# Tap positions and bias as two further products of the offset convolution, and four sampled tiles in flight

## The chip, the cores and the metric

The kernel runs on one core of a Trainium2 chip. The core has five engines that run their own instruction streams: TensorE (PE, matrix products, writing to the eight PSUM banks), VectorE (DVE), ScalarE (ACT), GpSimd (POOL) and SyncE (SP, which here only issues DMAs). They meet through semaphores. The metric is the device time of one execution in microseconds, as the median of several runs; less is better. A profile is taken in a separate execution.

## The reference, cut to what matters

Four layers run one after the other on an image batch `x` of shape (16, 32, 32, 32), each with a group norm before it and added to `x`: a mixture of experts on 2x2 patches, a deformable 3x3 convolution, a state-space layer, a depthwise 7x7 convolution with an MLP. The change lies in the second:

```python
om = _conv3x3(x, w_om, b_om)                # 27 channels: 9 dy, 9 dx, 9 masks
o1, o2, m = jnp.split(om, 3, axis=1)
offset = jnp.concatenate([o1, o2], axis=1)
mask = jax.nn.sigmoid(m)
dy = offset[:, 0::2]
dx = offset[:, 1::2]
base_y = (jnp.arange(H)[None, :, None] - 1 + ky.reshape(K2, 1, 1)).astype(jnp.float32)
base_x = (jnp.arange(W_)[None, None, :] - 1 + kx.reshape(K2, 1, 1)).astype(jnp.float32)
py = base_y[None] + dy
px = base_x[None] + dx
y0 = jnp.floor(py)
x0 = jnp.floor(px)
...                                         # four corners gathered, weighted, summed, times the mask
out = jnp.einsum('bckhw,ock->bohw', sampled, w.reshape(CO, C, K2))
```

So a sampling position is: a convolution with `w_om`, plus a bias `b_om` per channel, plus the place of the tap, which is the pixel's row (or column) plus the tap's own offset.

## The kernel before

The 16 images are worked in four **steps** of four images (NS = 4), and the partitions hold 4 images x 32 channels. Layers are staggered: while step s is in the deformable convolution, the experts of step s+1 and the state-space and depthwise layers of step s-1 run beside it. `order(step)` is a hand-made schedule: it gives every piece of work a place between 0 and 32, the numbers of the step's 32 gather tiles ("slots"), and each engine runs its own pieces in that one order. A piece late on one engine so holds back everything behind it on that engine.

**The deformable layer.** `head_a(a)` prepares the images of a pass a (passes 0, 1 and 2 are image 0, image 1, and images 2 and 3 of the first step; passes 3, 4 and 5 are whole steps). Its parts in order:

- `l1_norm`: DVE writes the normed image, with a border, to `xpad`.
- `l1_conv`: PE, nine products (one for each tap of the 3x3 window) with `w_om`, 108 output rows, of 512 columns for half an image's pixels (two pieces of 256 and one of 512 in pass 0); ACT copies the bank to `omt` (L1141).
- `l1_table`: PE transposes `xpad`, ACT copies, SP stores the table of corners to memory, from where POOL gathers.
- `l1_om`: PE transposes `omt` (L1764) so that pixels lie on the partitions; DVE adds the table `bb` of places and bias (L1451) and clips the positions to 0..33 (L1456) in `cw`.
- `l1_index` and `l1_share`: DVE floors the positions, makes the row numbers `idx` for the gather, and the corner weights `cw` from the fractions and the mask, whose tanh ACT makes (L1163).

`l1_conv` is written in pieces (`pieces(a)`): three in pass 0, two in each other pass, 13 in all. Passes 1 and 2 lie in the first step, at slots 3.2 to 5.5 and 11.9 to 15; passes 3 to 5 at slots 23.9 to 29 of the steps 0 to 2, for the next step. `load_conv` on DVE adds the bias to `bb` once (L1325).

**The tiles.** For each tile of 128 pixels of one image POOL issues nine indirect DMAs into `gt` (L1055), a ring of GRING = 4 places: the gathers of tile t wait until DVE has written `sm` of tile t-4. DVE's `sample` multiplies with the corner weights (L1508), adds twice (L1510), and writes the sampled tile to `sm` (L1516). `sm` is a ring of two places: this last instruction waits until PE has transposed the tile t-2 (`B1.filled(dve, "sampled", s, t - 2)`). PE's `turn` (L1772, at slot t+1) transposes `sm` into PSUM bank 3, ACT copies it to `st` (L1173), and `dcn` (L1783) multiplies with the weights after each group of tiles.

1152 gathers are issued in all (128 tiles of nine), from 78.2 us of the profiled execution to 1983.5 us.

## Time and profile before

| | |
|---|---|
| runs without a profile, us | 1748.33, 1746.49, 1748.08 |
| median, us | 1748.08 |
| span of the profiled execution, first to last instruction, us | 2176.8 |
| mean granted TensorE clock in it | 0.801 |
| PE / weight loads / DVE / ACT / POOL busy, us | 1392.0 / 595.6 / 953.2 / 526.5 / 1190.0 |
| DMA traffic | 123.70 MB, mean 57 GB/s |

The profiled execution is 428.7 us longer than the median. No record of what lies around its span stands in the profile, so the span is taken as its own time. Times of single instructions come from it; the sum of waits in it is not that of a run without a profile. In the granted clock 1.0 is 2.4 GHz and 0.5 is 1.2 GHz. A row of a timeline gives start, duration, engine, source line, operation, output<-input, the count, and in brackets how long the engine had been idle and what ended that ("issue": nothing that the profile shows; "remote": something it can't name).

### The profile page before, as it was taken

The numbers are of one execution on the slowest core, as the hardware profiler recorded it, in microseconds if no ns is written. First come the engines' busy times: TensorE is split into PE (matmuls) and PEld (weight loads), VectorE is DVE, ScalarE is ACT, GpSimd is POOL, SyncE is SP. The second block draws the span as 40 slices with busy tenths as digits, with TensorE's granted clock in tenths as the row PEclk, the third lists the DMA queues.
The fourth block names the chain that finished last, engine by engine and source line by source line (L and its number), as shares of the span: only waits on it lengthen the run. The fifth ranks groups of instructions, "written<-read, shape, count | busy, mean of one in ns | idle before, by whom it ended". The sixth has DMA issues, their size and how long they took to land.

```text
span 2176.8 us, 13143 instructions
## 1 busy us (share of the span) xinstructions
PE 1392.0 (64%) x3780; PEld 595.6 (27%) x3780; DVE 953.2 (44%) x1562; ACT 526.5 (24%) x860; POOL 1190.0 (55%) x1393
## 2 busy tenths in 40 slices
PE   4647554496246877863366878855368874386976
PEld 3433212242112333322122333322123321132322
DVE  2424233354341333884532323875323328532564
ACT  1111111121112233211222333211213322132544
POOL 8655446357665555676565454676645566673000
PEclk9868766698567998986577889977678987687987
DMA  5212212132241111222141111222221112110100
GB/s 192 60 48 68 52 40 62 49 90 59 74 101 41 43 44 43 71 66 58 53 113 46 31 40 39 74 65 58 57 76 35 41 44 57 41 58 26 32 5 18
DMA packets 111591, 123.70 MB, mean 57 GB/s; under 512 B 50720, under 2 KB 88224, under 8 KB 111136
## 3 DMA queue, kind: packets, MB, share of 16 engines
q0 software_dynamic: 36864, 75.57, 12.5%
q1 hardware_dynamic: 73600, 43.82, 8.1%
q10 hardware_dynamic: 1056, 3.47, 0.4%
q8 instruction: 31, 0.51, 0.1%
q14 instruction: 40, 0.33, 0.0%
HBM read 99.79 MB, written 9.01 MB: 50 GB/s over the span
## 4 chain that ended last, share of the span: by engine, by line
PE 36%; another core or an unknown queue 27%; DVE 16%; issue 12%; ACT 7%; DMA 1%; SPq 1%; ACTq 0%; DVEq 0%
PE bank L1795 7%; PE bank L1808 7%; PE bank L1721 4%; DVE rb L1599 3%; PE bank L1717 3%; PE bank L1731 3%; DVE gt L1508 3%; PE bank L1752 2%; PE bank L1831 2%; PE bank L1783 2%; PE bank L1817 1%; DVE he L1406 1%; PE bank L1847 1%; PE bank L1772 1%
## 5 line engine op out<-in xcount | busy, mean ns | idle before, releaser
L1055 POOL DMA_INDIRECT gt<-corner_table,idx x1152 | 1135.1, 985 | 783.8 <-DVE sm L1516 392.4
L1795 PE MATMUL bank<-u,wk 128*128 128x512 f32 x512 | 256.7, 648 | 25.6 <-issue 9.6
L1808 PE MATMUL bank<-yg,wts 128*128 128x512 f32 x512 | 241.6, 615 | 46.9 <-ACT yg L1189 30.2
L1406 DVE SCALAR_TENSOR_TENSOR he<-he,bank 128x512 f32<-128x512 f32 (+1 forms) x144 | 90.2, 627 | 275.4 <-remote 88.9
L1721 PE MATMUL bank<-xg,w_sb 128*128 128x512 f32 (+1 forms) x288 | 149.3, 602 | 85.0 <-DVE xg L1397 61.9
L1772 PE MATMUL bank<-cst,sm 128*128 128x128 f32 x384 | 80.0, 322 | 187.0 <-ACT st L1173 79.7
L1540 DVE SCALAR_TENSOR_TENSOR tg<-tg,ae 128x512 f32<-128x512 f32 x64 | 44.5, 696 | 344.3 <-ACT ae L1201 270.9
L1731 PE MATMUL bank<-he,w_sb 128*128 128x512 f32 (+1 forms) x288 | 143.0, 580 | 54.6 <-DVE he L1406 30.9
L1508 DVE TENSOR_TENSOR gt<-gt,bank 128x1152 f32<-128x1152 f32 x128 | 172.5, 1347 | 0.9
L1599 DVE SCALAR_TENSOR_TENSOR rb<-xp,par,rb 128x1024 f32<-128x1024 f32 x124 | 155.1, 1291 | 0.0
L1125 ACT ACTIVATE he<-bank 128x512 f32<-128x512 f32 (+1 forms) x144 | 78.8, 549 | 294.3 <-PE bank L1717 166.7
L1795 PEld LDWEIGHTS bank<-u,wk 128*128 128x128 f32 x512 | 102.5, 208 | 164.2 <-issue 149.3
L1717 PE MATMUL bank<-xp,w_sb 128*128 128x512 f32 (+1 forms) x288 | 145.4, 589 | 2.5 <-ACT he L1125 2.5
L1808 PEld LDWEIGHTS bank<-yg,wts 128*128 128x128 f32 x512 | 96.9, 196 | 167.3 <-issue 111.5
L1173 ACT ACTIVATE st<-bank 128x384 f32<-128x384 f32 x128 | 62.4, 487 | 266.0 <-remote 144.1
L1772 PEld LDWEIGHTS bank<-cst,sm 128*128 128x128 f32 x384 | 54.7, 164 | 262.6 <-issue 146.5
L1752 PE MATMUL bank<-xpad,wts 128*108 128x512 f32 (+1 forms) x234 | 103.5, 601 | 23.9 <-issue 13.1
L1510 DVE TENSOR_TENSOR gt<-gt 128x320 f32<-128x320 f32 (+1 forms) x256 | 106.0, 455 | 4.4
L1721 PEld LDWEIGHTS bank<-xg,w_sb 128*128 128x128 f32 x288 | 55.4, 206 | 160.8 <-DVE xg L1397 85.2
L1189 ACT ACTIVATE yg<-bank,cb 128x512 f32<-128x512 f32 x64 | 43.6, 684 | 221.8 <-remote 138.9
L1516 DVE TENSOR_TENSOR sm<-gt 128x288 f32<-128x288 f32 x128 | 58.6, 458 | 86.2 <-remote 82.0
L1847 PE MATMUL bank<-xp,musq 128*128 128x512 f32 x68 | 47.6, 852 | 73.6 <-issue 42.6
(222 smaller groups left out, 1390.2 us busy)
## 6 DMA issues: line engine op xcount, KB each, us to landing
gt<-corner_table,idx POOLq DMA_INDIRECT x1152
tb<-gate_of_token SPq DMA_DIRECT2D x32, 256.0 KB
sqb<-gate_of_token SPq DMA_DIRECT2D x24, 256.0 KB
u<-sqb SPq DMA_DIRECT2D x48, 128.0 KB
corner_table<-tb SPq DMA_DIRECT2D x36, 128.0 KB, 2.7
w_sb<-w ACTq DMA_DIRECT2D x2, 1024.0 KB, 6.7
sqb<-gate_of_token SPq DMA_DIRECT2D x16, 128.0 KB
u<-xg SPq DMA_DIRECT2D x16, 128.0 KB
```

Source lines behind the costliest of these rows:

```text
L1055: pool.indirect_dma_start(gt[:, t % GRING, k].rearrange("p a c -> p (a c)"), None, corners, bass.IndirectOffsetOnAxis(ap=idx[s % 2][:, j, ...
L1406: stt(out=he[:, u % 2, 0:w], in0=he[:, u % 2, 0:w], scalar=1.0, in1=psum[b][:, 0:w], op0=ALU.add, op1=ALU.mult).then_inc(free[b], 1)
L1508: ch.then(tt(rows, rows, share.unsqueeze(2).to_broadcast([P, 4 * KK, C]), ALU.mult))
L1510: ch.did(tt(gt[:, i, ks, 0:2], gt[:, i, ks, 0:2], gt[:, i, ks, 2:4], ALU.add))
L1599: op = stt(out=y, in0=win, scalar=weight, in1=y, op0=ALU.mult, op1=ALU.add)
L1717: mm(psum[b][:, 0:w], w1_sb[:, e, 2 + h], tokens(xpf, images), start=True, stop=True).then_inc(full[b], 1)
L1721: mm(psum[b][:, 0:w], w1_sb[:, e, h], xg[:, u // 2 % 2, 0:w], start=True, stop=True).then_inc(full[b], 1)
L1731: mm(psum[2][:, 0:w], w2_sb[:, e, h], he[:, u % 2, 0:w], start=first, stop=last)\
L1752: op = mm(psum[b][0:OMC, 0:(hi - lo) * P], w_om[:, k], xpad_v[:, y0:y1, k % 3:k % 3 + W], start=k == 0, stop=k == KK - 1)
L1772: op = pe.transpose(psum[3][:, k * P:(k + 1) * P], sm[:, t % 2, k * P:(k + 1) * P], ident)
L1795: op = mm(psum[b][:, :], wk[:, t, d], u4[:, g, at:at + HALF], start=t == 0, stop=t == JJ - 1 and n > 0)
L1808: op = mm(psum[B2.bank(*name)][:, :], w_glu[:, k, col + d * P:col + (d + 1) * P], yg[:, c % 2, k], start=k == 0, stop=k == NB2 - 1)
```

## The change

The table `bb` of 8 x 108 numbers for each partition becomes a weight of 108 columns. Rows 0 to 31 hold, for the 36 y columns, pixel row + tap row; rows 32 to 63, for the x columns, pixel column + tap column. `load_conv` adds the bias to the first 32 rows. `l1_conv` gets two further products into the same bank: one whose moving operand picks the pixel's row out of the identity matrix (each of its columns repeated 32 times), and one that picks the pixel's column (the 32 columns repeated for each row). Since exactly one of the first 32 rows is picked by the first product, the bias is added once. `l1_om` on DVE then no longer adds: it copies the mask out of the bank, and clips the positions straight out of the bank into `cw`. The self-wait on `om_ready` is gone, and `l1_index` waits for the bank's release instead. PE waits once for `bb` (`places_ready`) where it before waited for the weights alone.

The ring `sm` has four places instead of two, so the waits are on the transposes of tile t-4. `bb` shrinks by 756 numbers for each partition, `sm` grows by 768.

```diff
@@
+SRING = 4
@@
+def nth_tile(s, t):
+
+    return s * NT * GI + t
@@
-        bb = sb("bb", [P, NT, OMC])
+        bb = sb("bb", [P, OMC])
@@
-        sm = sb("sm", [P, 2, 3 * P])
+        sm = sb("sm", [P, SRING, 3 * P])
@@ def load_conv():   (DVE)
-                ch.did(tt(bb[:, :, :], bb[:, :, :], prm("b_om").unsqueeze(1).to_broadcast([P, NT, OMC]), ALU.add))
+                tt(bb[:, :], bb[:, :], prm("b_om"), ALU.add).then_inc(S["places_ready"], 1)
@@ def l1_om(a, halves):   (DVE)
-                    tt(own(a, om(a)[:, lo:hi], 3), own(a, got, 3), own(a, bb[:, lo:hi], 3), ALU.add).then_inc(free[b], 1)
-                for n in halves:
-                    B0.read(dve, "om", a, n)
-                pos = own(a, om(a)[:, tt_, 0:NXY], 2)
-
-                ts(pos, pos, 0.0, float(H + 1), ALU.max, ALU.min).then_inc(S["om_ready"], 1)
+                    mask = slice(2 * NK + ks.start, 2 * NK + ks.stop)
+                    op = ts(om(a)[:, lo:hi, mask], got[:, :, mask], 1.0, None, ALU.mult)
+                    if n == halves[-1]:
+                        op.then_inc(S["om_ready"], 1)
+                    ts(own(a, om(a)[:, lo:hi, 0:NXY], 2), own(a, got[:, :, 0:NXY], 2), 0.0, float(H + 1), ALU.max, ALU.min)\
+                        .then_inc(free[b], 1)
@@ def l1_index(a, halves):   (DVE)
-                dve.wait_ge(S["om_ready"], part(a, h) + 1)
+                for n in halves:
+                    B0.read(dve, "om", a, n)
@@ def sample(s, t):   (DVE)
-                if t >= 2:
-                    B1.filled(dve, "sampled", s, t - 2)
+                if t >= SRING:
+                    B1.filled(dve, "sampled", s, t - SRING)
                 elif s:
-                    B1.filled(dve, "sampled", s - 1, NT * GI + t - 2)
-                tt(sm[:, t % 2, 0:KK * C].rearrange("p (k c) -> p k c", k=KK), gt[:, i, :, 0], gt[:, i, :, 1],
+                    B1.filled(dve, "sampled", s - 1, NT * GI + t - SRING)
+                tt(sm[:, nth_tile(s, t) % SRING, 0:KK * C].rearrange("p (k c) -> p k c", k=KK), gt[:, i, :, 0], gt[:, i, :, 1],
@@ def load_conv():   (PE)
                 pe.wait_ge(S["wts_in"], 48)
+                pe.wait_ge(S["places_ready"], 1)
@@ def l1_conv(a, halves):   (PE)
-                                xpad_v[:, y0:y1, k % 3:k % 3 + W], start=k == 0, stop=k == KK - 1)
+                                xpad_v[:, y0:y1, k % 3:k % 3 + W], start=k == 0, stop=False)
+                    y0, y1 = lo * (P // W), hi * (P // W)
+                    mm(psum[b][0:OMC, 0:(hi - lo) * P], bb[:, :],
+                       ident[:, y0:y1].unsqueeze(2).to_broadcast([P, y1 - y0, W]), start=False, stop=False)
+                    op = mm(psum[b][0:OMC, 0:(hi - lo) * P], bb[:, :],
+                            ident[:, C:C + W].unsqueeze(1).to_broadcast([P, y1 - y0, W]), start=False, stop=True)
@@ def tap_places():
-    base = np.zeros((P, NT, 3, GI, KK), np.float32)
-    p, t, k = np.arange(P)[:, None, None], np.arange(NT)[None, :, None], np.arange(KK)[None, None, :]
-    base[:, :, 0] = (t * (P // W) + p // W + k // 3)[:, :, None]
-    base[:, :, 1] = (p % W + k % 3 + 0 * t)[:, :, None]
-    return base.reshape(P, NT * OMC)
+    base = np.zeros((GI, C, 3, GI, KK), np.float32)
+    at, k = np.arange(C)[:, None], np.arange(KK)[None, :]
+    base[0, :, 0] = (at + k // 3)[:, None]
+    base[1, :, 1] = (at + k % 3)[:, None]
+    return base.reshape(P, OMC)
@@ def lay_out(a):
-    put("b_om", np.broadcast_to(b_om[:, None], (3, GI, KK)).reshape(1, OMC).repeat(P, 0))
+    put("b_om", np.concatenate([np.broadcast_to(b_om[:, None], (3, GI, KK)).reshape(1, OMC).repeat(C, 0), np.zeros((P - C, OMC))]))
```

The order of the work is otherwise the same. On PE, in the first half of pass 2 (`he` stands for `omt`, `cst` for the identity), the stretch before reads:

```order
L1752 MATMUL bank<-xpad,wts 108x512 [waits bank0_free,xpad_ready]
L1752 MATMUL bank<-xpad,wts 108x512 x8
L1772 MATMUL bank<-cst,sm 128x128 [waits bank3_free,smp_ready]
L1772 MATMUL bank<-cst,sm 128x128 x2
L1741 MATMUL bank<-cst,xpad 128x128 [waits bank1_free,xpad_ready]
```

and with the change:

```order
L1760 MATMUL bank<-xpad,wts 108x512 [waits bank0_free,xpad_ready]
L1760 MATMUL bank<-xpad,wts 108x512 x8
L1763 MATMUL bank<-cst,bb 108x512
L1765 MATMUL bank<-cst,bb 108x512
L1785 MATMUL bank<-cst,sm 128x128 [waits bank3_free,smp_ready]
L1785 MATMUL bank<-cst,sm 128x128 x2
```

Two products of full width stand ahead of the tile's transposes and of those for the table. On DVE, at the same place, before:

```order
L1516 TENSOR_TENSOR sm<-gt 128x288 [waits bank3_full,dve_chain]
L1451 TENSOR_TENSOR cw<-bank,bb 128x12x18 [waits bank5_full]
L1456 TENSOR_SCALAR cw<-cw 128x4x2x18 [waits bank5_free]
L1465 CAST fl<-cw 128x8x18 [waits om_ready]
L1466 CAST fl<-fl 128x8x18 [waits dve_chain]
```

and with the change:

```order
L1523 TENSOR_TENSOR sm<-gt 128x288 [waits bank3_full,dve_chain]
L1458 TENSOR_SCALAR cw<-bank 128x4x18 [waits bank5_full]
L1461 TENSOR_SCALAR cw<-bank 128x4x2x18
L1472 CAST fl<-cw 128x8x18 [waits bank5_free]
L1473 CAST fl<-fl 128x8x18 [waits dve_chain]
```

As many instructions stand there, both now read the bank, and one of the waits between them is gone.

## Rows read from the trace of the kernel before

**Rows 1.** The page: busy time of each engine, and the chain that ended last.

```profile
PE 1392.0 (64%) x3780; PEld 595.6 (27%) x3780; DVE 953.2 (44%) x1562; ACT 526.5 (24%) x860; POOL 1190.0 (55%) x1393
...
PE 36%; another core or an unknown queue 27%; DVE 16%; issue 12%; ACT 7%; DMA 1%; SPq 1%; ACTq 0%; DVEq 0%
```

**Rows 2.** All gathers (one line of the program): durations, first and last start, idle before.

```profile
L1055 POOL DMA_INDIRECT gt<-corner_table,idx x1152: 938/944/2039, 78.2 to 1983.5; - x192
...
  DVE sm L1516: 392.4, 40
  issue: 359.1, 1108
...
  DMA corner_table<-rb: 12.1, 1
  DMA corner_table<-tb: 7.6, 2
```

**Rows 3.** POOL's timeline: two neighbouring gathers, the first after a wait.

```profile
1175.27 0.94 POOL L1055 DMA_INDIRECT gt<-corner_table,idx  x1 [1.42 <-DVE sm L1516]
1176.51 0.94 POOL L1055 DMA_INDIRECT gt<-corner_table,idx  x1 [0.30 <-issue]
```

**Rows 4.** Timelines of PE, ACT and DVE around the convolution of pass 4.

```profile
977.48 15.62 PE L1752 MATMUL bank<-xpad,wts 128*108 128x512 f32 x36
1019.09 0.60 ACT L1141 ACTIVATE he<-bank 108x512 f32<-108x512 f32 x1 [40.92 <-remote]
1022.72 0.60 ACT L1141 ACTIVATE he<-bank 108x512 f32<-108x512 f32 x1 [3.03 <-remote]
1022.84 0.46 DVE L1516 TENSOR_TENSOR sm<-gt 128x288 f32<-128x288 f32 x1 [27.82 <-remote]
```

**Rows 5.** POOL's timeline: the gather behind the second of DVE's three waits.

```profile
1023.57 1.75 POOL L1055 DMA_INDIRECT gt<-corner_table,idx  x1 [8.53 <-DVE sm L1516]
```

**Rows 6.** Pass 0, timelines of PE, DVE and POOL: the first piece, up to the first gather.

```profile
68.89 5.95 PE L1752 MATMUL bank<-xpad,wts 128*108 128x256 f32 x18 [0.86 <-DVE xpad L1425]
75.76 0.22 DVE L1451 TENSOR_TENSOR cw<-bank,bb 128x54 f32<-128x54 f32 x1 [4.14 <-PE bank L1764]
78.21 1.19 POOL L1055 DMA_INDIRECT gt<-corner_table,idx  x1 [12.64 <-DVE idx L1473]
```

**Rows 7.** Pass 1, timelines of PE and POOL: the first half, and tile 8's first gather.

```profile
171.13 9.88 PE L1752 MATMUL bank<-xpad,wts 128*108 128x512 f32 x18 [8.07 <-issue]
196.45 0.95 POOL L1055 DMA_INDIRECT gt<-corner_table,idx  x1 [12.08 <-DMA corner_table<-rb]
```

**Rows 8.** Chain that ended last, by time: two of five unnamed waits before pass 1.

```profile
115.88 10.80 another core or an unknown queue
...
131.98 8.69 another core or an unknown queue
```

**Rows 9.** Pass 2, timelines of PE, DVE and POOL: the first half and what waited.

```profile
318.16 9.76 PE L1752 MATMUL bank<-xpad,wts 128*108 128x512 f32 x18 [9.18 <-DVE xpad L1425]
329.52 0.38 DVE L1451 TENSOR_TENSOR cw<-bank,bb 128x216 f32<-128x216 f32 x1 [8.68 <-PE bank L1764]
337.22 0.94 POOL L1055 DMA_INDIRECT gt<-corner_table,idx  x1 [23.78 <-DVE sm L1516]
```

**Rows 10.** DVE's groups by shape: count, busy us, mean ns, idle before.

```profile
L1504 DVE TENSOR_SCALAR bank<-cw 128x288 f32<-128x288 f32 x14 | 6.4, 454 | 0.2
L1451 DVE TENSOR_TENSOR cw<-bank,bb 128x432 f32<-128x432 f32 x6 | 3.6, 608 | 7.3 <-PE bank L1764 7.0
L1456 DVE TENSOR_SCALAR cw<-cw 128x576 f32<-128x576 f32 x3 | 1.4, 461 | 0.3
L1504 DVE TENSOR_SCALAR bank<-cw 128x144 f32<-128x144 f32 x4 | 1.2, 301 | 0.2 <-DVE cw L1493 0.2
```

**Rows 11.** DVE's timeline: the table's bias, and the next instruction.

```profile
59.27 1.07 DVE L1325 TENSOR_TENSOR bb<-bb,par 128x864 f32<-128x864 f32 x1
63.28 1.20 DVE L1418 TENSOR_TENSOR X<-X,xg 32x512 f32<-32x512 f32 x1 [2.94 <-DMA xg<-fl]
```

More of the change, by code:

```diff
@@ L715, in build @@
             xn0_ready xp_in o_in max_ready exp_ready gate_ready gate_out patch_ready he_used
-            xpad_ready rows_ready om_ready mask_ready idx_ready smp_ready relu_done
+            places_ready xpad_ready rows_ready om_ready mask_ready idx_ready smp_ready relu_done
             u_ready glu_done sq_ready ln2_ready rstd2_ready x2_added
@@ L800, in loads @@
                 sp.dma_start(wts[:, :], weights).then_inc(S["wts_in"], 16)
-                sp.dma_start(bb[:, :, :].rearrange("p t m -> p (t m)"), places).then_inc(S["wts_in"], 16)
+                sp.dma_start(bb[:, :], places).then_inc(S["wts_in"], 16)
                 sp.dma_start(wenc[:, :], w_enc).then_inc(S["wts_in"], 16)
@@ L1444, in l1_om @@
             def l1_om(a, halves):
-                h, tt_, ks = span(a, halves)
+                h, at, ks = span(a, halves)
                 for n in halves:
@@ L1771, in turn @@
                 for k in range(3):
-                    op = pe.transpose(psum[3][:, k * P:(k + 1) * P], sm[:, t % 2, k * P:(k + 1) * P], ident)
+                    op = pe.transpose(psum[3][:, k * P:(k + 1) * P], sm[:, nth_tile(s, t) % SRING, k * P:(k + 1) * P], ident)
                 op.then_inc(full[3], 1)
```

## The prediction

> **What bounds the kernel now.** I read the page first: no engine is busy for two thirds of the span, and the largest share of the chain that ended last, 27%, is waits that end for no reason the profile can name [rows 1]. So the busy shares say little, and the question is who sets the pace. The next view is the one line of POOL's gathers. The reader is to see three sums in it [rows 2]: 1152 gathers, 392.4 us of idle time before 40 of them until DVE had written `sm`, and 359.1 us of "issue" before the others. The timeline gives the pace: one gather starts each 1.24 to 1.25 us (0.94 us, then 0.30 us) [rows 3]. So a tile of nine costs 11.25 us, and all 1152 cost about 1437 us at this pace.
>
> Put together, the profiled execution is 78.2 us before the first gather, 1905 us of gathering, and 192 us from the last gather at 1983.5 us to the end at 2176.8 us. If POOL never waited at all, that would be 78 + 1437 + 192 = 1707 us. The median of the runs is 1748.08 us. So in a run without a profile POOL may stand idle for only some 41 us between its first and its last gather, if the pace is the same there. In the profiled execution it is idle for 392.4 + 12.1 + 7.6 = 412 us. The 429 us by which the profiled span is longer thus lie about where POOL waits, and I take them for stalls that a normal run mostly lacks.
>
> What such a stall looks like matters for this change, because three of them lie right behind the convolution that grows. In pass 4 the rows of PE have both halves at 977.5 to 993.1 us, but ACT gets the first bank only at 1019.1 us and the second 3.6 us later, less than half the 7.8 us that nine such products take in the row; and DVE, which waits at `sm` for a transpose queued behind them, goes on at 1022.84 us [rows 4]. So PE's rows there don't show when the products were finished. The Trainium skill says the same of the row (Perfetto Trace Analysis, Tensor Engine Instruction): the end of a TensorE instruction is estimated by the profiler, not observed. By that rule, the rows give the work of a product, and not when ACT may have its bank; the trace agrees, by those 26 us.
>
> **Part 1, two more products for each piece.** 13 pieces get two products each. At the high clock 18 products of 512 columns take 15.62 us, 0.87 us each [rows 4]; nine of 256 take 5.95 us in pass 0, 0.66 us each [rows 6]; where PE had idled before, nine of 512 take 9.88 and 9.76 us, 1.1 us each [rows 7, 9]. The moving operand repeats elements, which no row shows for a product; I take the price of the neighbours, with a free product as the lower end and double the price as the upper. The whole addition is then: pass 0, 1.3 + 1.3 + 1.7 = 4.3 us at most (the second piece priced as the first); passes 1 and 2, 2.2 + 1.8 us each, 8 us; passes 3 to 5, 4 x 0.87 = 3.5 us each, 10.5 us; in all 23 us of PE work. What of it reaches the end depends on who waits for the piece.
>
> Pass 0: the first piece lies on the way to the first gather (PE, ACT, PE, DVE, then POOL, which had been idle for 12.64 us) [rows 6]. That is +1.3 us to POOL's start. The two later pieces are needed by POOL only two and four tiles later, at 11.25 us a tile, and hide.
>
> Pass 1: tile 8's gather waited 12.08 us for the corner table [rows 7], whose transposes stand behind the first half's products on PE. In the profiled execution its 2.2 us would be on the path. In a normal run POOL could have gathered eight tiles by 78 + 90 = 168 us at the earliest, whereas the table, at 196.45 us here, came after five unnamed waits of 37 us together between 102 and 141 us [rows 8]. Without those the table is there by 160 us, and the 2.2 us hide. The second half stands ahead of the next pass's expert products on PE and of DVE's work for them, and this stretch (32 units of three 0.86 us products in 5.4 slots, 83 us against 61 us of gathers) is one in which PE can't keep POOL's pace. So I count 1.8 us.
>
> Pass 2: POOL had waited 23.78 us, DVE 8.68 us for the transposed convolution, PE 9.18 us for `xpad` [rows 9]. With PE behind POOL's pace before it, this wait stays in a normal run, and the first half's 2.2 us lie on it; the second half hides behind 11.25 us of gathers.
>
> Passes 3 to 5: POOL stays four tiles (45 us) ahead of DVE. The next step's positions and table are due at slots 27 to 29, and POOL needs them only after tile 31, some 33 us after DVE's sample of tile 28. The added 3.5 us on a stretch of 15.6 us of PE fit in that. I take 0; the upper end is 10.5 us.
>
> Sum of part 1: the start's 1.3 us and the 1.8 + 2.2 us of the expert stretch overlap only partly, since PE's work follows the start too; 1.3 + 1.8 + 2.2 = 5.3 us. Lower end 1.3 us; upper end all 23 us.
>
> **Part 2, DVE.** In passes 3 to 5 two additions (608 ns) and a clip (461 ns), 1.68 us, become two copies of 144 numbers and two clips of 288 numbers out of a bank. No row reads a bank with that shape; the nearest write one, 301 ns and 454 ns [rows 10]. That gives 1.51 us, 0.2 us less for each pass, off the path. In passes 0 to 2 shapes are small and both versions are two instructions, with one semaphore turn less: below 0.1 us. The skill speaks against this part (VectorE: DVE Perf Modes, Why PSUM operands drop a tier): a clip of float32 numbers out of SBUF may use both read ports, one out of PSUM can't, so per number it is dearer than before. By the row 576 numbers take 461 ns and by that rule the same number out of a bank would take about half as long again, an estimate; at three passes it is below 1 us. The table's bias shrinks from 1.07 us to some 0.3 us, but DVE idles 2.94 us behind it for a DMA anyway [rows 11]. PE's new wait at `load_conv` is for that instruction, 8 us ahead of the first convolution. The table's load is 378 KB smaller and off the path. I count 0 for all of it, with -1 us as the lower end.
>
> **Part 3, four places in `sm`.** The wait for tile t-2 held DVE in three places (27.82 us the one shown), each behind a convolution of passes 3 to 5 [rows 4]. With four places DVE would pass it, but meets the wait for the transposed convolution two instructions or so later, which ended 3 us after. POOL gains the start of one more tile: it had been idle for 7.49, 8.53 and 8.15 us before the gathers behind the three, of which the second stands [rows 5], 24.2 us at most. Without the stall the gain is nothing: between transposes t-2 and sample t, DVE's own work of the slot needs later PE results, so PE has the old tile done by then; and after a convolution PE is behind by 15.6 + 3.5 = 19 us, less than two tiles. I take 0; the end on the good side is -24.2 us. POOL's first fill of `sm` doubles (0.7 us more) and the fill is awaited by nothing that was late.
>
> **Forecast:** 1748.08 + 5.3 = 1753.4 us, about +0.3%. Against the profiled execution's own 2176.8 us the same sum would be more, since pass 1's path counts there too.
>
> **Rivals.**
> (a) *All of it hides.* If POOL's idle 41 us lie elsewhere, only the start's 1.3 us remain, less the DVE's 1 us: 1748.4 us. For it: PE is idle a third of the span. Against it: the 23.78 us wait in pass 2 [rows 9].
> (b) *The ring frees POOL, and it is faster.* If the stalls behind the convolutions of passes 3 to 5 are real in a normal run, four places let POOL issue one tile more in each: -24.2 us, against 5.3 us of part 1 and the 10.5 us of passes 3 to 5, which then are on the path: 1748.08 - 24.2 + 15.8 = 1739.7 us. It decides from the point where PE's transposes are late by more than two tiles, 22.5 us. Against it: stalls of that size don't fit into 41 us together with pass 2's.
> (c) *The products are on the path everywhere.* If gathers are quicker in a normal run than 1.25 us, POOL gets ahead and waits for each pass's positions: up to 23 us, say 18 us without the hidden pieces of pass 0 and 2: 1766 us.
>
> **How the numbers follow.** A measurement can tell about 0.2%, 3.5 us, from no change. The forecast with its neighbours (+3.5 to +12 us) has 0.36, (a) 0.32, (b) 0.2, (c) 0.12. Faster by over 0.2% is (b) with a small part of (a), where DVE's release is worth more than I say: 0.21. Within is most of (a) and an edge of the forecast: 0.38. Slower is the rest: 0.41. The range reaches from (b) to (c): 1739 to 1766 us; outside are a ring that gains all 24.2 us and products of double price.
>
> **What would show it.** Right: in the changed profile 26 more pairs of products and about 23 us more PE work in the convolution's rows; the first gather 1 to 1.5 us later; DVE's group for the bank reads at some 1.5 us for each late pass; no wait of DVE at `sm`. Wrong: products with repeated elements at another price than 0.87 us; POOL's idle time until `sm` smaller by over 20 us, with fewer unnamed waits behind the convolutions, which speaks for (b); POOL waiting at the three later steps' starts for positions or the table, which speaks for (c).

## The result, and the profile after

The changed kernel takes 1754.77 us in the median (1754.08 to 1756.29), the kernel before 1748.08 us (1745.22 to 1749.17) beside it: a ratio of 1.0042, 95% interval 1.003 to 1.0055. It is slower, by about 7 us. Run again beside the kernel before (`change_again` below), it stood at 1.0035 [1.0022, 1.0048].

The profiled execution of before that the prediction rests on has a span of 2176.8 us, and nothing like it occurs in the runs. A second profiled execution of the unchanged kernel (`before_again` below) has 1745.9 us, so the comparisons here use it. The page of the changed kernel, busy times and chain:

```profile
span 1754.5 us, 13249 instructions
...
PE 1338.7 (76%) x3832; PEld 580.1 (33%) x3832; DVE 949.6 (54%) x1565; ACT 527.7 (30%) x860; POOL 1194.9 (68%) x1393
...
PE 41%; POOL 26%; DVE 12%; issue 11%; ACT 3%; SPq 3%; DMA 3%; ACTq 0%; POOLq 0%; DVEq 0%
```

The same of `before_again`:

```profile
span 1745.9 us, 13143 instructions
...
PE 1314.8 (75%) x3780; PEld 570.1 (33%) x3780; DVE 951.9 (55%) x1562; ACT 527.8 (30%) x860; POOL 1195.4 (68%) x1393
...
PE 47%; DVE 19%; POOL 15%; issue 8%; ACT 5%; DMA 3%; SPq 3%; ACTq 0%; POOLq 0%; DVEq 0%
```

PE is busy 23.9 us longer and the unnamed 27% of [rows 1] is gone in both. The span grew by 8.6 us. Where, is read from the one line of the gathers. First `before_again`, then the changed kernel: what ended POOL's idle time (total, times).

```profile
L1055 POOL DMA_INDIRECT gt<-corner_table,idx x1152: 940/945/2039, 77.9 to 1575.8; - x192
...
  issue: 348.9, 1145
  DVE idx L1473: 13.0, 1
  DVE sm L1516: 8.5, 5
  DMA corner_table<-rb: 0.3, 1
```

```profile
L1061 POOL DMA_INDIRECT gt<-corner_table,idx x1152: 940/944/2040, 79.3 to 1582.8; - x192
...
  DVE sm L1523: 15.3, 7
  DVE idx L1480: 14.8, 1
  DMA corner_table<-tb: 0.3, 1
```

The start is 1.4 us later, POOL waits 15.6 us in place of 8.8 between its first and its last gather (+6.8 us), and busy time and issue of the gathers together (1490.0 and 1488.7 us) and what follows the start of the last one (170.1 and 171.7 us) nearly cancel. Of the 412 us of waits of [rows 2], 403 us had been disturbance.

The waits have one place. POOL's timeline of `before_again`, rows with a wait for `sm` over 0.5 us:

```profile
353.64 1.27 POOL L1055 DMA_INDIRECT gt<-corner_table,idx  x1 [0.76 <-DVE sm L1516]
...
369.19 0.94 POOL L1055 DMA_INDIRECT gt<-corner_table,idx  x1 [4.04 <-DVE sm L1516]
...
383.24 0.94 POOL L1055 DMA_INDIRECT gt<-corner_table,idx  x1 [3.10 <-DVE sm L1516]
```

And all of the changed kernel:

```profile
331.02 0.94 POOL L1061 DMA_INDIRECT gt<-corner_table,idx  x1 [0.82 <-DVE sm L1523]
...
346.80 0.94 POOL L1061 DMA_INDIRECT gt<-corner_table,idx  x1 [4.73 <-DVE sm L1523]
...
359.88 1.27 POOL L1061 DMA_INDIRECT gt<-corner_table,idx  x1 [2.02 <-DVE sm L1523]
...
375.43 0.94 POOL L1061 DMA_INDIRECT gt<-corner_table,idx  x1 [4.04 <-DVE sm L1523]
...
389.47 0.94 POOL L1061 DMA_INDIRECT gt<-corner_table,idx  x1 [3.10 <-DVE sm L1523]
```

This is the experts' last pass of step 0, `units_a(3)`, placed at slots 16.3 to 22.5. PE is fully busy there (60.7 of the 61 us from 299 us in `before_again`), DVE takes PE's banks as they come and writes `sm` in between, and POOL follows. The later PE enters this stretch, the earlier POOL's lead of four tiles is used up. PE's first product of it starts at 299.34 us in `before_again` and at 306.50 us in the changed kernel.

How those 7.2 us arise, is seen behind pass 1. PE's timeline of `before_again`: both halves of the convolution, and the first expert product that waits behind them.

```profile
133.55 9.61 PE L1752 MATMUL bank<-xpad,wts 128*108 128x512 f32 x18 [8.06 <-DVE xpad L1425]
...
149.38 7.89 PE L1752 MATMUL bank<-xpad,wts 128*108 128x512 f32 x18
...
163.28 1.22 PE L1721 MATMUL bank<-xg,w_sb 128*128 128x512 f32 x2 [3.85 <-DVE xg L1397]
```

The same of the changed kernel, with the new products (L1763 the rows, L1765 the columns; each product has two records, as each of the nine has):

```profile
136.37 10.84 PE L1760 MATMUL bank<-xpad,wts 128*108 128x512 f32 x18 [8.05 <-DVE xpad L1431]
147.05 1.02 PE L1763 MATMUL bank<-cst,bb 128*108 128x512 f32 x2
147.91 1.02 PE L1765 MATMUL bank<-cst,bb 128*108 128x512 f32 x2
...
155.15 7.89 PE L1760 MATMUL bank<-xpad,wts 128*108 128x512 f32 x18
162.88 1.02 PE L1763 MATMUL bank<-cst,bb 128*108 128x512 f32 x2
163.73 1.02 PE L1765 MATMUL bank<-cst,bb 128*108 128x512 f32 x2
...
170.64 2.08 PE L1729 MATMUL bank<-xg,w_sb 128*128 128x512 f32 x2 [3.73 <-DVE xg L1403]
```

The start is 2.8 us later (pass 0's three pairs, 3.4 us of work, less what PE's pauses take up), the first half takes 1.2 us longer (mean granted clock 0.73 over it in place of 0.83; PE had idled 8 us ahead of both), and two pairs add 1.7 us each, start to start: 7.4 us.

Not all of that is the change's doing. The same program was profiled a second time (`change_again`), and there the first half takes as long as before, at a mean granted clock of 0.82:

```profile
136.10 9.67 PE L1760 MATMUL bank<-xpad,wts 128*108 128x512 f32 x18 [8.06 <-DVE xpad L1431]
...
169.13 2.08 PE L1729 MATMUL bank<-xg,w_sb 128*128 128x512 f32 x2 [3.66 <-DVE xg L1403]
```

Behind pass 1 PE is 5.9 us late in it, 2.5 us from pass 0 and the two pairs; these come with the change in both profiles. From there to the last pass some of the lateness is made up, as PE had idled 5.7 us for a sample at 219.6 us of `before_again` and idles 1.2 us there with the change: at the start of pass 2's convolution 5.4 us are left in the first profile and 1.0 us in the second, pass 2 adds its two pairs, and at the last pass it is 7.2 and 3.2 us. From 130 to 262 us the mean granted clock is 0.87 in the first and 0.90 in the second. So one program enters the last pass at two times 4 us apart.

### The profile page after: what moved, and what is told of

The parts are those of the page before. It is cut to its first block, busy times and chain, and to the rows that moved or that the text cites. A ratio compares the mean times of both kernels' runs of the same rounds, so it can differ in the third digit from the quotient of the medians.

```text
span 1754.5 us, 13249 instructions
## 1 busy us (share of the span) xinstructions
PE 1338.7 (76%) x3832; PEld 580.1 (33%) x3832; DVE 949.6 (54%) x1565; ACT 527.7 (30%) x860; POOL 1194.9 (68%) x1393
## 4 chain that ended last, share of the span: by engine, by line
PE 41%; POOL 26%; DVE 12%; issue 11%; ACT 3%; SPq 3%; DMA 3%; ACTq 0%; POOLq 0%; DVEq 0%
POOL gt L1061 26%; PE bank L1808 7%; PE bank L1821 6%; PE bank L1760 5%; PE bank L1729 5%; PE bank L1725 4%; PE bank L1739 4%; DVE gt L1515 2%; SPq L769 2%; PE bank L1860 2%; PE bank L1844 2%; PE bank L1796 1%; SPq L781 1%; PE bank L1785 1%; DVE rb L1606 1%
## 5 line engine op out<-in xcount | busy, mean ns | idle before, releaser
L1808 PE MATMUL bank<-u,wk 128*128 128x512 f32 x512 | 242.8, 619 | 12.4 <-DMA u<-sqb 6.8
L1821 PE MATMUL bank<-yg,wts 128*128 128x512 f32 x512 | 234.7, 602 | 3.2 <-DVE musq L1575 1.7
L1606 DVE SCALAR_TENSOR_TENSOR rb<-xp,par,rb 128x1024 f32<-128x1024 f32 x124 | 155.2, 1292 | 0.0
L1785 PE MATMUL bank<-cst,sm 128*128 128x128 f32 x384 | 75.2, 311 | 89.7 <-DVE sm L1523 87.1
L1808 PEld LDWEIGHTS bank<-u,wk 128*128 128x128 f32 x512 | 97.7, 198 | 138.5 <-issue 124.2
L1739 PE MATMUL bank<-he,w_sb 128*128 128x512 f32 (+1 forms) x288 | 136.4, 557 | 3.9 <-DVE he L1412 3.8
L1760 PE MATMUL bank<-xpad,wts 128*108 128x512 f32 (+1 forms) x234 | 106.2, 613 | 20.5 <-DVE xpad L1431 20.5
L1517 DVE TENSOR_TENSOR gt<-gt 128x320 f32<-128x320 f32 (+1 forms) x256 | 106.1, 456 | 4.4
L1739 PEld LDWEIGHTS bank<-he,w_sb 128*128 128x128 f32 x288 | 55.6, 195 | 63.0 <-issue 53.3
```

Source lines behind the costliest of these rows:

```text
L1517: ch.did(tt(gt[:, i, ks, 0:2], gt[:, i, ks, 0:2], gt[:, i, ks, 2:4], ALU.add))
L1606: op = stt(out=y, in0=win, scalar=weight, in1=y, op0=ALU.mult, op1=ALU.add)
L1739: mm(psum[2][:, 0:w], w2_sb[:, e, h], he[:, u % 2, 0:w], start=first, stop=last)\
L1760: op = mm(psum[b][0:OMC, 0:(hi - lo) * P], w_om[:, k], xpad_v[:, y0:y1, k % 3:k % 3 + W], start=k == 0, stop=False)
L1785: op = pe.transpose(psum[3][:, k * P:(k + 1) * P], sm[:, nth_tile(s, t) % SRING, k * P:(k + 1) * P], ident)
L1808: op = mm(psum[b][:, :], wk[:, t, d], u4[:, g, at:at + HALF], start=t == 0, stop=t == JJ - 1 and n > 0)
```

## The experiments

**before_again.** The kernel before, unchanged.

> The kernel before, unchanged, for a second profile. Theory (POOL's gathers set the pace; the unnamed waits of the first profile belong to that execution alone): the span comes out near 1746 us, POOL's idle time before gathers (without 'issue' and without the first wait) falls from 412 us to some 10 us, all of it in the stretch of the last expert pass of the first step, and DVE waits nowhere at sm. Rival (the unnamed waits are a part of the kernel): a span over 2000 us again.

Measured 1747.73 us with a span of 1745.9 us. Its rows are above. What follows: the long waits of [rows 2, 4, 5, 7 to 9] belong to that one execution, and POOL's idle time without them is 8.8 us. One part of the expectation missed: DVE does wait at `sm`, once, for 10.35 us (below).

**products_only.** The change with the ring of before.

```diff
-SRING = 4
+SRING = 2
```

> The changed kernel with two places in sm as before (SRING = 2), so the products and the DVE part alone. Theory (the ring is worth nothing, the products cost all): 1754 to 1755 us, +6 to +7 us on before, as the changed kernel. Rival (the ring gave something back or cost something): more than 2 us away from the changed kernel's 1754.8 us.

Measured 1758.04 us, 1.0056 [1.0034, 1.0078], span 1758.4 us, POOL's waits 17.5 us. The whole loss is there without the ring. The median lies 3 us above the range of the theory, where the rival had put it; whether the ring gives back the difference to 1.0042 can't be told, as the intervals overlap. With two places DVE waits at `sm` three times, 18.8 us in all, behind the convolutions of passes 3 to 5, and with four never; but POOL has no wait over 0.5 us in steps 1 to 3 in either profile. DVE's timeline of `products_only`, the longest:

```profile
436.68 0.46 DVE L1523 TENSOR_TENSOR sm<-gt 128x288 f32<-128x288 f32 x1 [14.13 <-PE bank L1785]
```

**ring_only.** The kernel before with four places in `sm`, `bb` shrunk to hold the first tile's places alone (so all tiles get sampling positions around the first tile's, and the output isn't the reference's).

```diff
+SRING = 4
-        bb = sb("bb", [P, NT, OMC])
+        bb = sb("bb", [P, OMC])
-                if t >= 2:
-                    B1.filled(dve, "sampled", s, t - 2)
+                if t >= SRING:
+                    B1.filled(dve, "sampled", s, t - SRING)
```

> The kernel before with four places in sm. To make room, bb holds the places of the first tile only and is added, repeated, by the same instructions, so sampling positions of later tiles are others than in the reference; the work is the same in number and size. Theory: within 2 us of before (1746 to 1750 us). Rival (ring helps): 5 us or more faster.

Measured 1.0002 [0.9986, 1.0017], span 1745.6 us, POOL's waits 8.5 us. For the kernel before the ring is worth nothing that can be measured. DVE's timeline of `before_again` shows the only wait at `sm` that there was to remove, behind pass 3's convolution; POOL had no wait behind it:

```profile
424.50 0.46 DVE L1516 TENSOR_TENSOR sm<-gt 128x288 f32<-128x288 f32 x1 [10.35 <-PE bank L1772]
```

**pair_again_early, pair_again_late, pair_again_pass0, pair_again_pass2.** The change with the pair issued once more ahead of the pieces of some passes. The convolution restarts the bank, so the result stays. The condition is the only thing that differs: `a < SPLIT` (passes 0 to 2), `a >= SPLIT` (3 to 5), `a == 0`, `a == 2`.

```diff
+                    if a < SPLIT:
+                        y0, y1 = lo * (P // W), hi * (P // W)
+                        mm(psum[b][0:OMC, 0:(hi - lo) * P], bb[:, :],
+                           ident[:, y0:y1].unsqueeze(2).to_broadcast([P, y1 - y0, W]), start=True, stop=False)
+                        mm(psum[b][0:OMC, 0:(hi - lo) * P], bb[:, :],
+                           ident[:, C:C + W].unsqueeze(1).to_broadcast([P, y1 - y0, W]), start=False, stop=True)
                     for k in range(KK):
```

> The changed kernel with the pair of products issued once more in passes 0 to 2, ahead of the nine of the convolution (the convolution then starts the bank anew, so the result is the same). Theory (the pairs of the first step all lie on PE's chain up to the experts' last pass, where POOL waits): the pieces there hold 2 x (0.43 + 0.43 + 4 x 0.86 + 0.86) = 10.3 us of products, of which those of the last half of pass 2 and the pieces that DVE or ACT overlap may hide, so +6 to +10 us on the changed kernel. Rival (only the 1 us of POOL's start reaches the end): +1 us.

Measured 1.01 [1.008, 1.012], 10 us above the change's ratio of 1.0042. The first gather stays at 79.3 us: the repeated pair runs ahead of the first piece's nine products, and these then take 4.7 us in place of 6.8 us. The rest of it is on the path.

> The changed kernel with the pair of products issued once more in passes 3 to 5, ahead of the nine of the convolution, which starts the bank anew. PE gets 6 x 2 x 0.86 = 10.3 us more, the same amount as in pair_again_early. Theory (in the last slots of a step PE is idle and POOL four tiles ahead): within 2 us of the changed kernel, 1753 to 1757 us, POOL's waits unchanged at 15 us. Rival (each late pass is on the path too): +10 us.

Measured 1.0088 [1.0072, 1.0105], 8 us above the change. The theory that a second pair hides in the late passes missed. POOL's waits are 21.4 us in place of 15.6 us; 3.6 us of the new ones stand in step 2, where the experts and the depthwise taps both need DVE. That leaves over half of the 8 us without a place in the trace.

> The changed kernel with the pair issued once more in pass 0 alone, 2 x (0.43 + 0.43 + 0.86) = 3.4 us of products. Theory (pass 0's later pieces hold up DVE, which holds up the experts' products of pass 1, and so on to the experts' last pass): POOL's wait there grows by 2 to 3 us, and so does the time, though the first gather comes less than 1 us later. Rival (only the first gather counts): 0 to +1 us, POOL's waits unchanged.

Measured 1.0069 [1.005, 1.0088], about 5 us above the change, where I had expected 2 to 3; the two intervals overlap, so the size is rough. POOL's waits for `sm` are those of the change. But a new wait stands at its first gather of pass 2, 2.7 us over the usual 0.30 (POOL's timeline; the profile can't name what ended it):

```profile
266.64 0.94 POOL L1061 DMA_INDIRECT gt<-corner_table,idx  x1 [3.00 <-issue]
```

SP's timeline suggests what it waited for, the table of pass 2, whose nine DMAs (start, and how long their issue took) end 3.1 us ahead of it (`idx` had been written 6 us ahead):

```profile
257.44 6.07 SPq L876 DMA_DIRECT2D corner_table<-rb  x9
```

In the changed kernel they end 3.3 us ahead of the gather (262.48 us), without a wait:

```profile
253.36 5.86 SPq L876 DMA_DIRECT2D corner_table<-rb  x9
```

And in `before_again` 9.3 us ahead of it (261.32 us):

```profile
246.28 5.75 SPq L870 DMA_DIRECT2D corner_table<-rb  x9
```

So in this profile the change used up some 6 us of cover at this place. How little is left can be bounded: in `pair_again_early` the gather follows the end of the table's issue by 2.0 us, here by 3.1 us, so 0.2 to 1.3 us were left. In `change_again` the gap is 7.5 us, and most of the cover is still there.

> Changed kernel with the pair of products issued once more ahead of both pieces of pass 2 (the convolution restarts the bank, so the results stand): 3.5 us more PE work, in the place where my prediction put 2.2 us of cost for the first half. Theory 'pass 2 hides, since POOL waits for sm only in the experts' last pass of the step, whose start depends on PE's total delay until then': +2 to +3.5 us over the changed kernel, all of it in POOL's waits for sm between 320 and 400 us, and no wait of POOL at pass 2's start. Rival 'pass 2's first half is on the path by itself': a wait of POOL for idx or the corner table at the start of pass 2. Second rival 'it hides altogether': within 1 us.

Measured 1.0055 [1.0042, 1.0068], beside the change's 1.0035 on the same chip: +3.5 us by the ratios, the upper end of the first theory. The size is rough, since the intervals overlap and the medians (1758.55 and 1751.63 us) are 6.9 us apart. The place is clear: no wait at pass 2's start, and the waits for `sm` between 320 and 400 us grew to 19.4 us, from 14.7 and 12.7 us in the change's two profiles.

The kernels in one table, all in us. "Last pass" is PE's first product of the experts' last pass, "table" the end of issue of pass 2's table, "waits" POOL's waits for `sm` over 0.5 us in the last pass.

| kernel | last pass | table | first gather of pass 2 | waits | span |
|---|---|---|---|---|---|
| before_again | 299.34 | 252.03 | 261.32 | 7.9 | 1745.9 |
| ring_only | 299.68 | 251.98 | 261.68 | 7.9 | 1745.6 |
| change_again | 302.53 | 253.16 | 260.64 | 12.7 | 1748.9 |
| change, first profile | 306.50 | 259.22 | 262.48 | 14.7 | 1754.5 |
| products_only | 307.01 | 259.37 | 263.06 | 16.0 | 1758.4 |
| pair_again_late | 307.53 | 258.72 | 263.53 | 15.7 | 1761.9 |
| pair_again_pass2 | 309.47 | 259.35 | 262.51 | 19.4 | 1757.0 |
| pair_again_pass0 | 310.94 | 263.51 | 266.64 | 14.7, and 2.7 at pass 2 | 1758.9 |
| pair_again_early | 318.60 | 268.34 | 270.34 | 20.7, and 6.3 at pass 2 | 1766.1 |

PE's lateness at the last pass goes over into waits nearly one to one, within some 2 us in every row: against `before_again`, 4.8 us of waits for 3.2 us in `change_again`, 8.1 for 7.7 us in `products_only`, 11.5 for 10.1 us in `pair_again_pass2`. Where POOL has waited at pass 2 already, less is left for later: the sum counts, 19.1 us for 19.3 us in `pair_again_early`.

The two times of entry show here too. Six profiles have one pair up to this place: four enter at 306.5 to 307.5 us (the change's first, `products_only`, `pair_again_late`, and `after_wide` below), two at 302.5 and 302.9 us (`change_again`, `wide_pair_again_late`).

**before_wide and after_wide.** If that stretch is the limit, it should be spread. `units_a(3)` gets 7.9 slots in place of 6.2, what follows it in step 0 moves back; on the kernel before and on the change.

```diff
-        put(units_a(3), (16.3, 22.5))
+        put(units_a(3), (16.3, 24.2))
...
-        put([("l0_collect", a)], (22.6, 22.7))
-        put([("l0_tail", a)] + head_a(a), (23.9, 24.2, 2), (24.8, 29, len(head_a(a)) - 1))
+        at = 1.5 if step == 0 else 0
+        put([("l0_collect", a)], (22.6 + 1.2 * at, 22.7 + 1.2 * at))
+        put([("l0_tail", a)] + head_a(a), (23.9 + at, 24.2 + at, 2), (24.8 + at, 29 + at, len(head_a(a)) - 1))
```

> The kernel before with the experts' last pass of the first step spread over slots 16.3 to 24.2 instead of 22.5, and what follows it in that step moved by 1.5 slots. PE's work is the same; only DVE's samples come earlier among the experts' products. Theory (POOL's only wait is for samples that DVE has queued behind that pass): POOL's 8 us of waits go, 1737 to 1741 us. Rival (the wait moves to the start of the next step, whose positions now come 1.5 slots later): no gain, POOL waits for idx or the table there.

Measured 1742.22 us, 0.9963 [0.9951, 0.9976], span 1737.3 us. It beats both kernels, by a little less than expected; 2.1 us of POOL's 8.8 us of waits are left. POOL's waits, of which the first lies ahead of the first gather:

```profile
POOL gt L1056 <- DVE idx L1474: 13.1, 1, 13.1
POOL gt L1056 <- DVE sm L1517: 1.5, 5, 0.3
```

> The changed kernel with the same spread. Theory (the change costs by delaying the experts' last pass, and by 1.4 us at the first gather): the 15 us of waits go as well, and it comes within 2 us of before_wide plus 1.4 us: 1739 to 1743 us. Rival (the products cost somewhere else too): over 4 us above before_wide.

Measured 1748.41 us, 0.9992 [0.9979, 1.0005]: the loss is gone, but 6.2 us remain to `before_wide` (5.1 us by the ratios), above the theory's range, and the rival was right that something else costs too. In the traces 1.0 us is the start, and 1.7 us are POOL's waits: a new one of 1.8 us at the change to step 1, where it waits for the table, and one of 1.4 us for `sm`, less small ones. The other difference, 8.9 us more busy time and issue of the gathers, is nowhere near an edit. That sum lies between 1486.9 and 1496.0 us in the twelve profiles other than the disturbed one and that of `no_pairs`, and not in the order of the products they hold: the lowest is `pair_again_pass2`'s, the highest this one's. So the traces place 2.7 us of the cost and leave the rest open.

**change_again.** The changed kernel once more, to see what one profiled execution is worth.

> The changed kernel, unchanged, beside the kernel before on the chip of the other two kernels of this call. Theory 'the gathers' own sum differs from one profiled execution to the next by a few us, without a cause in the program': about 1.004 to 1.005 times the kernel before, the first gather at 79 to 80 us, POOL waits for sm of 15 to 16 us in the last expert pass of the first step as before, and a sum of busy time and issue between the gathers anywhere from 1487 to 1496 us. Rival 'that sum belongs to the program': it is 1488.7 us again, within 1 us, and the span is 1754 to 1755 us.

Measured 1.0035 [1.0022, 1.0048], span 1748.9 us where the first profile had 1754.5 us: first gather 1.4 us earlier, waits 2.0 us and the end 2.5 us shorter, gathers' sum 1489.1 us against 1488.7 us. The forecast of a start at 79 to 80 us and 15 to 16 us of waits missed; the sum stayed, as the rival said, but the rival's span of 1754 to 1755 us missed too, and two executions don't settle it. The runs show the same two times as the profiles: three take 1750.8 to 1751.6 us at a mean granted clock of 0.876 to 0.877, two take 1756.1 to 1756.4 us at 0.873 and 0.875. The profiled run is the shortest of its five (1750.76 us), that of the first profile was the longest of its own (1756.29 us). Differences of 5 us between two single profiles are within what one program shows; what is said above of mechanisms rests on waits that appear at a named place, and of costs on the timed ratios.

**wide_pair_again_late.** `after_wide` with the pair again in passes 3 to 5.

> Changed kernel with the first step's last expert pass spread over 7.9 slots in place of 6.2, and the pair of products once more in passes 3 to 5 (10.5 us more PE work). Against the changed kernel with the same spread, which took 0.9992 times the kernel before. In pair_again_late the milestones of POOL gave the late pairs 1.8 us in each of steps 0 and 1, 4.5 us in step 2 (of which two waits for sm, 3.6 us, at 1074 to 1088 us) and 1.0 us in step 3. Theory 'late pairs cost only where step 2's experts and the depthwise taps crowd DVE, about 3.6 us': +3 to +5 us, so 1.001 to 1.002 times the kernel before, with those two waits in the trace again. Rival 'they cost PE time throughout, by the shorter lead of PE in every step': +8 us or more, 1.004. Second rival 'the cost in pair_again_late was scatter': within 1.5 us of the spread kernel.

Measured 1.0033 [1.0023, 1.0044], 7 us above `after_wide`. POOL's timeline, all waits over 0.5 us after the first gather:

```profile
449.83 1.22 POOL L1062 DMA_INDIRECT gt<-corner_table,idx  x1 [4.37 <-DMA corner_table<-tb]
...
1062.09 0.94 POOL L1062 DMA_INDIRECT gt<-corner_table,idx  x1 [3.88 <-DVE sm L1524]
...
1074.95 1.74 POOL L1062 DMA_INDIRECT gt<-corner_table,idx  x1 [1.55 <-DVE sm L1524]
```

The two waits of step 2 stand before the same two gathers, the 757th and the 766th, as those of `pair_again_late` (2.09 us at 1074 and 1.54 us at 1087 us), so they are no scatter; the one for the table is 2.6 us longer than in `after_wide`. Together 8 us: the size lies between both theories, the places fit the first with one added.

Two limits. The spans of the two profiles are only 1.2 us apart (1749.7 and 1748.5 us): 6.6 us more waits in all are met by 4.3 us less busy time and issue of the gathers, and a start 1.1 us earlier. And the same two gathers of step 2 wait in `no_pairs` below (2.71 and 1.54 us), which has no added product at all, and in no other undisturbed profile. So that stretch is near its limit, and another delay than that of the pairs can show there. The wait for the table comes with the spread, which moved the table's work by 1.5 slots: in `pair_again_late`, without the spread, its issue ends 11.1 us ahead of step 1's first gather.

**no_pairs.** The change without the 26 products.

```diff
-                                xpad_v[:, y0:y1, k % 3:k % 3 + W], start=k == 0, stop=False)
...
+                                xpad_v[:, y0:y1, k % 3:k % 3 + W], start=k == 0, stop=k == KK - 1)
```

> The changed kernel with all 26 added products left out and everything else of the change kept (DVE reads the bank with a copy and a clip, the table's short load, four places in sm). Without them the positions hold neither grid nor bias, so the output isn't the reference's and all samples come from near one corner of the image. Theory 'the products alone cost the time': the kernel before's time within 0.15%, the first gather 0 to 0.5 us from that of the kernel before, waits for sm of 8 to 9 us in the first step's last expert pass. Rival 'DVE's new form or the wait of PE for the bias costs too': over 1.0015, that is 2.6 us or more. Rival 'DVE's new form saves': under 0.9985.

Measured 1796.3 us, 1.0273 [1.025, 1.0296]. No theory had this, and the experiment says nothing on DVE's part: with all positions near one corner the gathers themselves became slow to land (below), and the waits that grew are for DMAs, such as 20.9 us for pass 1's table. What DVE's new form costs by itself stays open, but for the start, where no gather runs yet: the first gather comes at 78.01 us, within 0.1 us of `before_again`, as the theory had it.

## Why the prediction was right, and where its steps were not

The forecast was 1753.4 us, +0.3%, for products on the path in step 0 and nothing elsewhere. The total stands (+0.35 and +0.42%), and so does the mechanism in its outline: work on PE that in step 0 isn't covered by POOL, and none seen in the later steps. Of the steps:

- **What bounds it.** Right that POOL's gathers set the pace and that the unnamed stalls don't occur in the runs. Wrong in the sum "78 + 1437 + 192 = 1707": the gathers need 1490 us, 1.29 us each and not 1.25, as some take up to 2 us, and the end takes 170 us: 78 + 1490 + 169 = 1737 us. Of the 41 us in which POOL could stand idle, 8.8 us were real. The pace came from the two neighbours of [rows 3], although [rows 2] show a longest gather of 2039 ns; the end came from the disturbed execution, where it is 23 us longer.
- **Price of the products.** Right at the high clock. In the changed kernel, PE's groups by shape:

```profile
L1763 PE MATMUL bank<-cst,bb 128*108 128x512 f32 x22 | 11.2, 592 | 0.0
...
L1763 PE MATMUL bank<-cst,bb 128*108 128x256 f32 x4 | 1.2, 379 | 0.0
```

  The neighbours L1760 have 639 and 470 ns. Repeated elements in the moving operand change nothing: start to start a new product of 512 columns takes 0.86 us, as each of the nine ahead of it does. All 26 take 20.6 us so. PE's busy time grew by 23.9 us in the first profile and by 16.0 us in `change_again`, on either side of that, as all of PE's work takes longer or shorter by the clock granted to it; the 23 us of the forecast met the first by luck. The dearer prices for the first pieces, 2.2 and 1.3 us a pair, weren't met: the pairs stand last in their piece, where the granted clock was 1.0 (at 75.1, 147.1 and 250.1 us), and took 1.7 and 0.9 us. The sign "26 more pairs of products" is a slip for 13 pairs; PE has 52 more records, two for each of 26 products.
- **Pass 0.** The start: +1.4 us against +1.3 us, which is luck in part, as the second profile of the change has +0.1 us. Over the seven profiles with one pair in pass 0 the first gather comes at 78.0 to 79.8 us, 79.2 us in the mean, and over the five without added products at 77.7 to 78.8 us, 78.1 us in the mean: +1.0 us. Pass 0 in the changed kernel, PE's timeline:

```profile
68.45 6.81 PE L1760 MATMUL bank<-xpad,wts 128*108 128x256 f32 x18 [1.30 <-DVE xpad L1431]
75.10 0.59 PE L1763 MATMUL bank<-cst,bb 128*108 128x256 f32 x2
75.53 0.59 PE L1765 MATMUL bank<-cst,bb 128*108 128x256 f32 x2
```

  The pair is 0.9 us of it, and the nine products took 6.8 us, against 5.7 us in `before_again` and 5.6 us in `change_again`, at mean granted clocks of 0.60, 0.72 and 0.74. The step "the two later pieces are needed only two and four tiles later, and hide" failed: POOL isn't late for them, but PE is, and passes the delay on to pass 1's start, 2.8 and 2.5 us in the two profiles.
- **Pass 1.** The step "without those the table is there by 160 us, and the 2.2 us hide" holds for POOL, and fails for the same reason. I counted the second half alone, 1.8 us; both, 3.4 us, arrive at the first expert product behind them. The 1.2 us by a lower clock belong to the first profile alone.
- **Pass 2.** The step "this wait stays in a normal run" failed: [rows 9]'s 23.78 us has no counterpart. Pass 2's products cost by another way: `pair_again_pass2` shows +3.5 us by the ratios for 3.5 us of work, with waits for `sm` 80 us and more later. I had given both halves 2.2 us.
- **The sum.** 5.3 us from three terms at partly wrong places, against 8.2 us of start and waits in the first profile and 4.9 us in the second (6.1 to 7.3 us in the timed ratios). It came near by luck, because two errors met. I left out some 4 us of passes 0 and 1; and of what arrives, PE's idle time takes a part. In the first profile PE is 7.4 us late behind pass 1, 5.4 us at pass 2's convolution (240.08 us against 234.66 us), would be 8.9 us late behind it, and is 7.2 us late at the last pass, as its four long idle times on the way there sum to 25.6 us in place of 27.8 us. The second profile loses 4 us more of it on the way (above), so neither figure is the price of the products alone.
- **Passes 3 to 5.** "I take 0" holds as far as the runs show, for one pair. The added work does fit ahead of POOL's need: SP's and POOL's timelines of the changed kernel, the table for step 1 and the first gather from it:

```profile
437.73 7.33 SPq L882 DMA_DIRECT2D corner_table<-tb  x9
...
459.48 0.94 POOL L1061 DMA_INDIRECT gt<-corner_table,idx  x1 [0.31 <-issue]
```

  The table's issue ends 14.4 us ahead of it, where `before_again` has 18.5 us, and 21.7 and 20.9 us ahead of those of steps 2 and 3; POOL doesn't wait there. A second pair in each late pass takes 3 to 5 us of that, and still costs some 8 us, of which 3.6 us are placed. So a cost of the first pair that leaves no wait can't be ruled out.
- **Part 2.** Six copies and six clips as forecast, 303 and 448 ns against 301 and 454 (DVE's groups in the changed kernel):

```profile
L1461 DVE TENSOR_SCALAR cw<-bank 128x288 f32<-128x288 f32 x6 | 2.7, 448 | 0.0
...
L1458 DVE TENSOR_SCALAR cw<-bank 128x144 f32<-128x144 f32 x6 | 1.8, 303 | 22.1 <-PE bank L1777 22.1
```

  The Trainium skill's rule (VectorE: DVE Perf Modes, Why PSUM operands drop a tier) had the direction for the wide clips: the 576 numbers take 896 ns in the two clips, where the one out of SBUF took 503 ns in `before_again`. A part of that is the second instruction; by the step from 144 to 288 numbers out of the bank (298 to 448 ns) one clip of 576 would take some 750 ns, an estimate, half as long again as 503. At 144 numbers no difference shows, 298 ns out of the bank and 304 ns out of SBUF. Off the path, and not isolated beyond the start.
- **The ring.** Right to count nothing: with the products it spares DVE 18.8 us of waits, none of which had reached POOL. Rival (b) rested on [rows 4, 5], and fell with them.

## What to carry over

Take a second profile when the first one's span is far from the runs, before any wait in it is used; its durations held here, its waits didn't. Then take two of the changed kernel as well: here they differ by 4 us in the very lateness that explains the cost. Ask of added work not only whether its own consumer can wait, but what stands behind it on the same engine: a delay that hides at each hand-over adds up on the busiest engine, and surfaces where that engine has no gap left. There spreading the dense stretch over more slots gave 0.4%, about what the change cost.

## What the runs showed of the hardware

**Gathers of near addresses land slowly.** With all positions in one corner (`no_pairs`) the gathers move the same bytes, but the time of their packets is four times that of the change. The DMA queues, share of the span of 16 engines; first `no_pairs`, then `change_again`:

```profile
q0 software_dynamic: 36864, 75.57, 62.8%
```

```profile
q0 software_dynamic: 36864, 75.57, 15.0%
```

That is 0.49 against 0.11 us for a packet of 2 KB (share x 16 x span / packets). `ring_only`, with positions around one tile, has 14.8%. How near they must be was not varied. An experiment that makes up the positions can so measure its own gathers in place of what it leaves out.

**Which DVE instructions go with a long gather.** 176 of the changed kernel's gathers take over 1.0 us, together 52 us more than 0.945 us each. They can be sorted by what DVE was doing when they started, by the timelines:

| DVE at the gather's start | gathers | over 1.0 us |
|---|---|---|
| idle | 519 | 1 |
| an instruction that reads a PSUM bank | 241 | 1 |
| one that reads a single tensor, from SBUF | 59 | 14 |
| one that reads two tensors, both from SBUF | 333 | 160 |

The last row has the write of `sm` (L1523, 45 long gathers), the depthwise taps (L1606, 34) and the additions of the samples (L1517, 27). In `change_again` 153 of 328 are long in it, and 1 of 248 in the second. DVE and POOL, from the timeline:

```profile
1082.60 1.28 DVE L1606 SCALAR_TENSOR_TENSOR rb<-xp,par,rb 128x1024 f32<-128x1024 f32 x1
...
1083.20 1.50 POOL L1061 DMA_INDIRECT gt<-corner_table,idx  x1 [0.30 <-issue]
```

The gather ends 0.82 us after the end of the tap under way at its start. So do, within 0.03 us, 115 of the 118 long gathers whose two-tensor instruction has a row of its own, as if they began their work there. The Trainium skill (SBUF — State Buffer, SBUF: two separate sides) says that VectorE and GpSimd share a port pair as an exclusive lock, which a DVE instruction takes in a two-port mode, or, against a GpSimd operation that reads SBUF, with two SBUF inputs. The counts agree with it for two SBUF inputs. That the lock is the cause was not tried; no run took such an instruction away.
